# A second-stage MLP, two attentions and a last MLP in separate stages, and the same work as one run of sixteen rounds

## The reference

```python
# end of layer 2
h = layer_norm(x, ln_mlp_scale, ln_mlp_offset)
x = x + gelu_exact(h @ w_fc1 + b_fc1) @ w_fc2 + b_fc2        # 256 -> 1024 -> 256
# layer 3
h = layernorm(x, ln1_s, ln1_b)
q, k, v = split(h @ w_qkv + b_qkv)
x = x + merge(attention(q, k, v, ltor_mask)) @ w_ao + b_ao    # 16 heads of 16
h = layernorm(x, ln2_s, ln2_b)
k, v = split(encoder @ w_kv + b_kv)
x = x + merge(attention(h @ w_q + b_q, k, v, cross_mask)) @ w_co + b_co
h = layernorm(x, ln3_s, ln3_b)
x = x + gelu_tanh(h @ w1 + b1) @ w2 + b2                      # 256 -> 1024 -> 256
# attention: scores = q k^T / 4; scores * mask - 10000 * (1 - mask); softmax; @ v
```

## Time and profile before

| | |
|---|---|
| runs | 1375.06, 1370.78, 1374.92 us, median 1374.92 |
| profiled execution | 1375.67 us, its span 1373.8 us |
| PE busy | 1269.7 us, 92% of the span, 8912 matmul records |
| DVE, ACT, POOL busy | 830.5 (60%), 746.3 (54%), 540.5 us (39%) |
| mean granted PE clock | 0.973 |
| `in_l_self` weights | issued at 1041.03 us, landed in 4.7 us |
| first PE record of the second half of `m2` | 1070.31 us |

### The profile page before, as it was taken

One profiled execution on the slowest core, in us unless ns is written; L12 is line 12 of the kernel. 1 busy time (PEld: TensorE's weight loads), 2 busy tenths in 40 slices (PEclk: granted clock), 3 DMA queues, 4 the chain that ended last, 5 costly groups with the idle time before them and its releaser, 6 DMA issues.

```text
span 1373.8 us, 24470 instructions
## 1 busy us (share of the span) xinstructions
PE 1269.7 (92%) x8912; PEld 1012.4 (74%) x8912; DVE 830.5 (60%) x1900; ACT 746.3 (54%) x2040; POOL 540.5 (39%) x571
## 2 busy tenths in 40 slices
PE   6999999999898988999999999999998977787788
PEld 5777777777644557899999889999985645545555
DVE  4666666766648976666666766666673039639510
ACT  4665656665546875555454655555543147647531
POOL 3554444544359963232130413221202039449320
PEclk9999999999997999999999999999999998988989
DMA  6101010100010004111111202020001010000000
GB/s 255 49 26 51 26 51 26 51 26 28 3 64 0 1 1 140 32 48 31 47 45 35 63 16 70 9 70 16 9 1 62 0 62 1 1 16 1 1 8 23
DMA packets 15525, 50.44 MB, mean 37 GB/s; under 512 B 1840, under 2 KB 5296, under 8 KB 14384
## 3 DMA queue, kind: packets, MB, share of 16 engines
q1 hardware_dynamic: 15408, 48.87, 10.8%
HBM read 47.82 MB, written 1.05 MB: 36 GB/s over the span
## 4 chain that ended last, share of the span: by engine, by line
PE 80%; DVE 12%; ACT 3%; issue 2%; POOL 2%; DMA 0%; SPq 0%; DVEq 0%; POOLq 0%
PE pS L1648 13%; PE acc L315 6%; PE pT L1676 6%; PE acc L1728 6%; PE pC L378 5%; PE pT L365 5%; PE pS L348 4%; PE pS L1690 4%; PE acc L334 4%; PE pC L1713 4%; DVE stats L1299 4%; PE acc L921 3%; PE pT L1452 2%; PE acc L1438 2%; PE pC L1452 2%
## 5 line engine op out<-in xcount | busy, mean ns | idle before, releaser
L1648 PE MATMUL pS<-split_sources,split_pair_weights 128*128 128x512 f32 x768 | 212.6, 412 | 5.8 <-issue 4.3
L665 POOL TENSOR_TENSOR probs<-probs,stats 128x512 f32<-128x512 f32 x128 | 130.6, 1042 | 167.0 <-DVE stats L543 166.9
L486 ACT ACTIVATE probs<-pS,stats 128x256 f32<-128x256 f32 x256 | 118.1, 473 | 111.1 <-DVE stats L538 111.1
L1648 PEld LDWEIGHTS pS<-split_sources,split_pair_weights 128*128 128x128 f32 x768 | 136.4, 191 | 30.8 <-issue 6.6
L1825 ACT ACTIVATE probsT<-pT 128x256 f32<-128x256 f32 x128 | 49.3, 385 | 197.0 <-PE pT L1701 197.0
L1728 PE MATMUL acc<-l_wo_parts,l_ctx_parts 128*128 128x256 f32 x768 | 122.0, 295 | 1.0 <-DVE l_ctx_parts L1897 1.0
L1676 PEld LDWEIGHTS pT<-l_wv_parts,split_sources 128*128 128x128 f32 x756 | 106.9, 188 | 14.2 <-issue 2.2
L1676 PE MATMUL pT<-l_wv_parts,split_sources 128*128 128x256 f32 x756 | 110.6, 281 | 2.1 <-issue 2.1
L1951 POOL TENSOR_TENSOR split_pair_weights<-weights_a,split_pair_weights 128x1024 fp32r<-128x1024 f32 x16 | 38.1, 2381 | 170.0 <-ACT split_pair_weights L1789 169.9
L315 PE MATMUL acc<-split_sources,split_pair_weights 128*128 128x512 f32 x372 | 101.9, 408 | 0.9 <-POOL split_pair_weights L652 0.7
L1728 PEld LDWEIGHTS acc<-l_wo_parts,l_ctx_parts 128*128 128x128 f32 x768 | 99.4, 190 | 1.2 <-DVE l_ctx_parts L1897 1.2
(11 more groups left out here) (206 smaller groups left out, 2979.1 us busy)
## 6 DMA issues: line engine op xcount, KB each, us to landing
weights_a<-in_l_w SPq DMA_DIRECT2D x16, 768.5 KB, 4.2
weights_a<-in_l_w SPq DMA_DIRECT2D x16, 768.0 KB, 5.9
value_bias_rows<-in_l_bv SPq DMA_DIRECT2D x16, 256.0 KB, 4.5
weights_b<-in_l_wo SPq DMA_DIRECT2D x16, 256.0 KB, 2.7
w_fc<-in_l_w SPq DMA_DIRECT2D x4, 1024.0 KB, 6.0
bias_rows<-in_rows SPq DMA_DIRECT2D x1, 1536.0 KB, 13.6
x_residual<-in_x_dbl SPq DMA_DIRECT2D x2, 512.0 KB, 7.1
masked_scores<-in_ctx_dbl SPq DMA_DIRECT2D x2, 512.0 KB, 8.0
```

Source lines behind the costliest of these rows:

```text
L486: a = e.activation(self.E[:, n % 4, h, it, :], self.S[h][:, it, :], ACT.Exp, bias=self.st[:, 1, n % 4, h, it:it + 1], accum_out=self.st[:, ...
L665: e.tensor_tensor(self.E[:, n % 4, h, :, :], self.E[:, n % 4, h, :, :], self.st[:, 3, n % 4, h, :].unsqueeze(2).broadcast_to([P, 2, D]), A ...
L1648: mm = e.matmul(bank[:, :], self.w_qk[i % 2][kw][:, 1 - which, c, h * P:h * P + P], g.split[:, which, ks, c, half * HALF:half * HALF + HAL ...
```

## The change

The nine stages become one, `LastLayer`. The first half of `m2` stays as it was. Then come the pieces of FIRST and a loop of 26 steps over sixteen rounds (eight of each attention), in which each step ends with the pieces that FILL names for it. A piece is: G a hidden block of `m2`'s second half, U its output for one batch, T the norm's transposes for a couple of batches (0 to 3 ahead of the first attention, 4 to 7 ahead of the second, 8 to 11 ahead of the last MLP), K and Q the keys and queries of a couple, V the values of a couple, J a block of 512 key columns from the context, H two hidden blocks of the last MLP for a couple (Gelu on 256 columns each), O its output for one batch. STATS and ROWS place the norm's statistics and rows on DVE; POOL takes 1/std and the bias addition in the same or the next step.

```diff
+    FIRST = ['G0', 'T0', 'G1', 'T1', 'G2', 'K00', 'Q00', 'V00', 'G3', 'K01', 'Q01', 'V01', 'G4']
...
+    STATS = {2: [2], 4: [3], 6: [4], 8: [5], 10: [6], 12: [7], 14: [8], 16: [9], 18: [10], 20: [11]}
```

The order on PE, with the bank claims (`last_use` holds what frees a bank; scores claim all four):

```diff
+        def scores(r):
...
+            for k in range(4):
+                self.claim(e, k, (self.scaled, 2 * r + 1 + k // 2))
...
+        for t in range(self.STEPS):
+            if 0 <= t - 4 < self.R:
+                back_transposes(t - 4)
+            if 0 <= t - 0 < self.R:
+                scores(t)
+            if 0 <= t - 3 < self.R:
+                context(t - 3)
+            if 0 <= t - 5 < self.R:
+                rows_transposes(t - 5)
+            if 0 <= t - 2 < self.R:
+                transposes(t - 2, 0)
+            for p in self.FILL.get(t, []):
+                self.pe_piece(e, p)
+            if 0 <= t - 5 < self.R:
+                attention_output(t - 5)
+            if 0 <= t - 2 < self.R:
+                transposes(t - 2, 1)
```

On ACT the first eight heads keep their single exponentials, and heads 8 to 15 are now one activation after POOL's shift, which has two parts instead of one and waits for both maxima:

```diff
+            if half == 0:
+                e.wait_ge(self.nmax, 2 * r + 1)
+                for n in range(8):
...
+            else:
+                e.wait_ge(self.shifted, 2 * r + 2)
+                a = e.activation(s[:, 1024:2048], s[:, 1024:2048], ACT.Exp)
...
+        def shift(r, c):
+            e.wait_ge(self.nmax, 2 * r + 2)
```

866 lines of the change are left out of this document (583 added, 283 removed).

## The result

| | before | after |
|---|---|---|
| runs of this comparison | 1375.06, 1370.78, 1374.92, 1371.59 us | 1349.58, 1347.79, 1347.80, 1351.65 us |
| median | 1373.26 us | 1348.69 us |
| span of the profiled execution | 1373.8 us | 1347.8 us |
| mean granted PE clock | 0.973 | 0.989 |

The ratio is 0.9826, with a 95% interval from 0.9805 to 0.9848: faster by 24.6 us. Forecast were 1332 us and a range up to 1350, so the direction was right, the time lies just inside the range, and 17 us of the forecast gain of 43 did not come. The rest of this text is about those 17 us.

The account below looks back on a forecast made before the run. GpSimd's loop (shifts, mask additions, maxima; 8.3 us) was taken to bound a step; 1070.3 + 21.2 + 68.4 + 83 + 80.7 + 2.6 = 1326.2, plus 3 clock and 1.5 hand-offs: span 1331, forecast 1332 us, range 1312 to 1350.

Parts of the forecast that it names:

- Part 2: Needs of one step: GpSimd's loop of shifts, mask additions and maxima, 8.3 us; even steps add 1.0; rows 0.66.
- Part 1: FIRST, up to step 0: 20.0 us of matmuls plus 1.2 of waiting for T1's rows, 21.2 us.
- Part 3: Steps 0 to 6, loaded and unsteady: lengths 4.9, 6.5, 12.5, 12.7, 7.7, 13.3, 10.8, together 68.4 us.
- Part 4: Steps 7 to 15: step 7 8.4, two pairs at 19.0, two at 17.6; 81.6, or 83 by TensorE's starts.
- Part 5: Steps 16 to 25: matmuls 72.0 plus waits 8.7, 80.7 us, with five table loads of 1.28.
- The clock: 3 us added to the sum for a slow clock, since steps 1 and 2 have waits of 2 to 3 us.
- (b): Rival: banks, shared output bank, late statistics lock steps; even 11.5, odd 9.5 us; about 1352; chance 0.17.
- Its sign: TensorE idle in steps 7 to 15, released by VectorE's add or bank evacuation, over 1.5 us a step: then (b).
- The other sign: GpSimd waiting more than 2 us a step, in which case its loop is not the bound.
- (a): Rival: TensorE nearly full, VectorE and GpSimd run ahead, only Part 5's waits remain; about 1308; chance 0.12.
- (c): Rival, slower than before: TensorE's fill and VectorE's chain do not overlap, steps 15.7 us; about 1432; chance 0.03.
- (d): Rival: borders vanish but clock falls to 0.90 in the rounds, costing about 7 us; chance 0.68 with the forecast.

Follow-up runs that it names:

- All together: On the changed kernel: output first, second transposes behind T in five steps, context copy early but behind T's copy, rows between maxima, bias later, fills reordered; 1331.99 us.
- the best order: Changed kernel with output first, Q behind second transposes, context copy early, rows between maxima, bias later: 1338.54 us; steps 7 to 15 81.8 us, as in All together.
- the output alone: Changed kernel with TensorE doing the attention output of round t-5 ahead of the step's fill instead of behind it; 1346.09 us, steps 7 to 15 86.6 us.

## Why the prediction came out as it did

The time fell inside the range, and its direction was right, but the bound that the sum rests on, GpSimd's loop (Part 2), was not the bound. That the time lies inside is partly luck: 3.1 us came from the stretch ahead of the change, at a clock that had been low in the trace I worked from. Without them it would be about 1351.8, above 1350.

**Part 1** (21.2 us): 22.2. TensorE waits 1.05 us for the rows of T1 where 1.2 was forecast, but two terms cancel in that: the second pair of rows takes 1.67 us, not 0.66, beside GpSimd's bias addition, and the work of G0, T0 and G1 left to do when the add has ended is 3.3 us, not 2.6. The other 1.0 us is a wait for the Gelu of G4 ahead of step 0's scores, which the working left out. Step 0 began at 1089.5 because FIRST began earlier.

**Part 2** failed in three terms. Rows were taken at 0.66 us from a stretch in which GpSimd was idle and moved beside its additions; two cost 2.24. The bias addition was taken at nothing because it fell into GpSimd's waits; it took 1.33 and did so fall, but it kept VectorE's rows blocked. And the loop "cannot be shortened", true in itself, was taken for the bound: GpSimd is busy 63.23 of 79.7 us from step 8 on, 79% where I wanted 85, and what I called idle only for the maxima was mostly waiting for maxima that came late. Taking a microsecond a round out of it left steps 8 to 12 as long as they were. The scores of steps 8 to 15 stand 9.9 us apart, where the loop wanted 9.2.

**Part 3** (68.4 us, measured 76.6): steps 1 and 2 have the slow clock that I only allowed for in a lump, G6 and G7 at 5.40 us instead of 3.60 and U4, U5 at 8.52 instead of 7.07:

```profile
1097.37 5.40 PE L1287 MATMUL heads_scores<-hT,w_fc 128*128 128x512 f32 x8 [1.34 <-DVE probs L2308]
1108.46 8.52 PE L1298 MATMUL heads_scores<-w_fc,hidden_b 128*128 128x256 f32 x32
```

Steps 3 and 5 each have the 1.11 us between T and K that my working left out. "All together" takes 3.7 us out of steps 3, 5 and 6 by order; steps 1 and 2 run as slowly as before in it.

**Part 4** (83 us, measured 91.0) is where the wrong bound cost most: the steps were priced by GpSimd's loop, with TensorE "closer behind". I gave TensorE 5.7 us plus fill and never wrote down its odd step in order. Done so, it is 8.3 us of matmuls, and rows, T, its copy on ScalarE, and Q in a row with nothing between, which makes 11.3. Of the 9.2 us lost against the best order (81.8), 4.3 go with the output alone, 1.6 of them by the clock of step 13.

**Part 5** (80.7 us, measured 88.0): the five table loads are there, each 1.28 us, and the activation starts at the load's end:

```profile
1263.22 1.28 ACT L1292 ACT_TABLE_LOAD   x1
1264.52 0.84 ACT L1292 ACTIVATE hidden_b<-heads_scores,bias_cols 128x256 f32<-128x256 f32 x2
```

The drain of 1.38 us that the Trainium skill adds (ScalarE: Activation LUTs, What ACT_TABLE_LOAD costs) is not seen here: the activation ahead of this load ended at 1263.20. In step 17 the waits are 1.48 and 1.68 (forecast 1.4 and 1.9), in step 18 1.17 (0.85 twice). T10 waits 1.72, not 2.7, but waits of 0.68 and 1.18 us for VectorE stand ahead of it in the same step. Left out were those and the low clock in steps 16 and 19 (context 1.93 us for 1.08; T10, O1 and O2 1.11 + 8.12 for 0.60 + 7.07).

**The clock**: 3 us were added for it. In the changed kernel the groups that ran slow add up to 8: 1.8 and 1.45 in steps 1 and 2, 1.64 in step 13 (Q13, 3.63 us instead of 1.99), 1.6 in step 16 (context 0.85, its row transposes 0.25, transposes 0.46) and 1.6 in step 19. So this term was right in kind and mis-sized.

```profile
1234.33 3.63 PE L1983 MATMUL heads_scores<-hT,weights_c 128*128 128x256 f32 x8 [1.11 <-ACT hT L2148]
1258.30 1.93 PE L2080 MATMUL heads_context<-heads_probsT_b,big 128*32 128x128 f32 x32 [0.61 <-DVE heads_probsT_b L2323]
```

**Rivals.** (b), steps locked to one another at 1352, came nearest in time. Its even steps should have been the long ones (11.5 and 9.5); it is the odd ones (9.5 and 11.3), and the lock is in TensorE's and ScalarE's queues, not in the output bank. Its sign did not come: of TensorE's idle time in steps 7 to 15 only one wait, of 1.4 us, was released by VectorE's add, and with all waits for copies out of PSUM banks (hT 4.4, probsT 3.5, heads_contextT 0.9) it comes to 1.1 us a step, below the 1.5 named. The add itself waits 1.40 us in odd and 1.85 in even steps for the output behind the fill, but that is VectorE's idle time. The other sign came: GpSimd waits more than 2 us a step. (a) and (c) did not happen: TensorE is neither nearly full nor without overlap. (d) happened, in single pieces and not over all rounds. Its 7 us were reckoned too low: with the two levels of the clock a granted mean of 0.90 means a fifth of the time at the low one, which by that reckoning is about 15 us in 151.

The change's own aim held: the waits at the borders (3.43 us for rows, a clock of 0.50) are gone. Of the 22.9 us, TensorE's busy time gives about 10 (244.6 us before, 234.2 now, at a granted clock of 0.92 and 0.97) and its idle time about 13. That both come from the borders and the rounds' own gaps is a reading of the windows; no run undid the merging alone.
